# Cross-attention and quantised FFN: FFN bias, residual sum and Wo's low part handed from VectorE to GpSimd

## The reference

```python
x = x + attention(layernorm(x), context) @ Wo + bo
x = x + ffn(layernorm(x))
...
# attention: q = ln(x Wq + bq), k = ln(y Wk + bk), v = y Wv + bv, 16 heads of 32;
# softmax(q k / sqrt(32)) v over 112 keys, plus the same over the 16 dca keys
...
bq = fake_quant(bias, RHS_BITS, -1)
xq = fake_quant(x, LHS_BITS, -1)
kq = fake_quant(kernel, RHS_BITS, 0)
y = jnp.einsum('bsd,df->bsf', xq, kq)
y = y + bq[None, None, :]
y = jax.nn.relu(y)
return fake_quant(y, LHS_BITS, -1)
```

## Time and profile before

| | |
|---|---|
| Time, median of 3 runs | 354.7 us (354.21 to 355.06) |
| Profiled execution | 354.8 us |
| Its span, first to last instruction | 353.0 us |
| Mean granted clock of TensorE | 0.991 |
| PE busy | 321.9 us, 2375 matmuls |
| PEld busy | 254.4 us |
| DVE busy | 315.7 us, 804 instructions |
| ACT busy | 221.9 us, 444 instructions |
| POOL busy | 173.8 us, 261 instructions |

### The profile page before, as it was taken

How to read it: one execution, slowest core, us unless ns; L and a number is a source line. 1 busy time by engine, 2 the same in 40 slices (tenths; PEclk the granted TensorE clock), 3 DMA queues, 4 the chain that set the end, 5 groups by cost and what they waited for, 6 DMA issues and landing times.

```text
span 353.0 us, 7629 instructions
## 1 busy us (share of the span) xinstructions
PE 321.9 (91%) x2375; PEld 254.4 (72%) x2375; DVE 315.7 (89%) x804; ACT 221.9 (63%) x444; POOL 173.8 (49%) x261
## 2 busy tenths in 40 slices
PE   5799989998999999999999999999999999987871
PEld 1355658776788888887878887878787878775630
DVE  3999899998889999999999999999999999986665
ACT  3577886375576767676768585858585856572401
POOL 5211712264373828282828282828383837272720
PEclk9999999999899999999999999999999999999998
DMA  7880345132151514251515151424233313130002
GB/s 268 255 302 3 120 134 185 46 122 78 46 151 46 174 41 153 67 170 49 172 43 178 49 169 58 153 74 147 81 130 97 122 63 121 64 130 22 26 6 89
DMA packets 36451, 38.88 MB, mean 110 GB/s; under 512 B 8760, under 2 KB 27452, under 8 KB 36412
## 3 DMA queue, kind: packets, MB, share of 16 engines
q1 hardware_dynamic: 36044, 38.14, 33.2%
q10 hardware_dynamic: 368, 0.27, 0.3%
HBM read 16.89 MB, written 4.72 MB: 61 GB/s over the span
## 4 chain that ended last, share of the span: by engine, by line
PE 59%; POOL 8%; DVE 7%; issue 5%; ACT 2%; DMA 1%; POOLq 0%; DVEq 0%; ACTq 0%
PE bank L1334 33%; PE bank L1457 9%; POOL finals L536 5%; PE bank L1437 3%; PE bank L1438 3%; PE bank L1629 2%; PE bank L1426 2%; PE bank L1511 2%; PE bank L1516 1%; PE bank L1478 1%; POOL x_small L593 1%; DVE seg_out L1079 1%; PE bank L1619 1%; DVE rden L1073 1%; ACT prob_store L757 1%
## 5 line engine op out<-in xcount | busy, mean ns | idle before, releaser
L517 POOL TENSOR_TENSOR k_lo<-wkv_raw,k_hi 128x448 f16<-128x448 f32 x16 | 16.8, 1049 | 109.4 <-issue 101.5
L1457 PE MATMUL bank<-v_aug,prob_store 128*128 128x66 f32 x512 | 67.1, 274 | 2.1 <-ACT prob_store L757 2.1
L1457 PEld LDWEIGHTS bank<-v_aug,prob_store 128*128 128x128 f32 x512 | 63.1, 191 | 4.5 <-ACT prob_store L757 3.2
L768 ACT ACTIVATE wkv_raw<-bank,affine 128x448 f32<-128x448 f32 (+1 forms) x32 | 22.3, 748 | 40.7 <-PE bank L1511 40.7
L1066 DVE TENSOR_REDUCE neg_max<-bank 128x4 f32<-128x448 f32 (+1 forms) x128 | 44.9, 412 | 0.3 <-PE bank L1426 0.3
L757 ACT ACTIVATE prob_store<-bank,exp_scale 128x512 f32<-128x512 f32 x64 | 41.7, 678 | 4.9 <-PE bank L1438 4.8
L536 POOL TENSOR_TENSOR finals<-seg_out 128x128 f32<-128x128 f32 x64 | 34.5, 548 | 12.6 <-DVE seg_out L1079 12.2
L1437 PE MATMUL bank<-q_stack,k_stack 128*128 128x128 f16 x256 | 33.9, 220 | 0.6 <-ACT maxT L612 0.6
L1438 PE MATMUL bank<-maxT,sel 128*128 128x128 bf16 x256 | 33.7, 219 | 0.0
L1079 DVE TENSOR_TENSOR seg_out<-bank,rden 128x256 f32<-128x256 f32 x64 | 27.2, 425 | 4.0 <-POOL finals L536 1.7
L1437 PEld LDWEIGHTS bank<-q_stack,k_stack 128*128 128x128 f16 x256 | 26.4, 104 | 5.2 <-issue 3.9
(11 more groups left out here) (213 smaller groups left out, 886.2 us busy)
## 6 DMA issues: line engine op xcount, KB each, us to landing
x_in<-in_x SPq DMA_DIRECT2D x16, 256.0 KB, 3.0
q_stack<-q_hi SPq DMA_DIRECT2D x32, 128.0 KB, 2.1
q_stack<-q_lo SPq DMA_DIRECT2D x32, 128.0 KB, 2.1
k_stack<-k_hi SPq DMA_DIRECT2D x32, 128.0 KB, 2.1
k_stack<-k_lo SPq DMA_DIRECT2D x32, 128.0 KB, 2.1
out<-finals SPq DMA_DIRECT2D x16, 256.0 KB, 2.0
y_dcaT<-in_x SPq DMA_DIRECT2D x8, 256.0 KB, 2.8
x_res<-in_x SPq DMA_DIRECT2D x8, 256.0 KB, 2.8
```

The source lines that it names most:

```text
L768: s.activation(n.rearrange("p (c n) -> p c n", n=P)[:, :, 0:keys], src, ACT.Identity, bias=shift, scale=gain).then_inc(n_ready.sem, 1)
L1457: last = mm(bank[6 + gr % 2][:, VW * h:VW * (h + 1)], probs[:, gr % 2, h], v_aug[:, Bt.parity, HG * gr + h], start=True, stop=True)
```

## The change

Three pieces of one-off work go from VectorE to GpSimd or to another place there. `low_output` becomes four subtractions of 128x512 on GpSimd in step 0, behind k's low part of batch 1. Of `setup_ffn_bias`, VectorE keeps the largest magnitude, the scale and its reciprocal and does them in step 1 behind the statistics of the second layer norm instead of ahead of the maxima; GpSimd waits for them (`fbstat_ready`) and does the two 128x512 operations ahead of k's low part of batch 2. The sum of x and the output bias of batch 0 goes from ahead of combine(0) to behind combine(3), on GpSimd as before.

```diff
-        pow2_ready = signal("pow2_ready")
+        pow2_ready, fbstat_ready, fbrnd_ready = signal("pow2_ready"), signal("fbstat_ready"), signal("fbrnd_ready")
...
+            def setup_ffn_bias():
+
+                pool.wait_ge(fbstat_ready.sem, 1)
+                g.tensor_scalar(fb_row[:], fb_row[:], fb_stat[:, 2:3], ROUND, ALU.mult, ALU.add).then_inc(fbrnd_ready.sem, 1)
+                pool.wait_ge(fbrnd_ready.sem, 1)
+                g.tensor_scalar(fb_row[:], fb_row[:], ROUND, fb_stat[:, 1:2], ALU.subtract, ALU.mult
+                                ).then_inc(fbias_ready.sem, 1)
+
+            def low_output():
+                pool.wait_ge(wohi_ready.sem, 1)
+                for c in range(XC):
+                    ins = g.tensor_tensor(wo_lo[:, c], wo_raw[:, c], wo_hi[:, c].bitcast(FP32), ALU.subtract)
+                ins.then_inc(wolo_ready.sem, 1)
...
                         dca_columns(k_hi, kdca_hi)
                         dca_columns(k_lo, kdca_lo)
+                        if C is not None and C.first():
+                            setup_ffn_bias()
                         low(k_lo, k_n, k_hi, kn_ready, khi_ready, kstack_in, klo_ready, MAIN)
+                        if N.second():
+                            low_output()
...
-                if Bt is not None:
+                def residual():
                     if Bt.first():
                         pool.wait_ge(out_bias_ready.sem, 1)
                     pool.wait_ge(*xres_loaded.of(Bt))
                     if Bt.has(1):
                         pool.wait_ge(*x1_ready.of(Bt.back(1)))
                     g.tensor_tensor(x_plus, x_res[Bt.parity], out_bias[:], ALU.add).then_inc(xplus_ready.sem, 1)
+
+                if Bt is not None and not Bt.first():
+                    residual()
...
                     combine(2)
                     combine(3)
+                    if Bt.first():
+                        residual()
...
-            def low_output():
-                dve.wait_ge(wohi_ready.sem, 1)
-                v.tensor_tensor(wo_lo[:], wo_raw[:], wo_hi[:].bitcast(FP32), ALU.subtract).then_inc(wolo_ready.sem, 1)
...
-                link(v.reciprocal(fb_stat[:, 2:3], fb_stat[:, 1:2]))
-                link(v.tensor_scalar(fb_row[:], fb_row[:], fb_stat[:, 2:3], ROUND, ALU.mult, ALU.add))
-                v.tensor_scalar(fb_row[:], fb_row[:], ROUND, fb_stat[:, 1:2], ALU.subtract, ALU.mult
-                                ).then_inc(fbias_ready.sem, 1)
+                v.reciprocal(fb_stat[:, 2:3], fb_stat[:, 1:2]).then_inc(fbstat_ready.sem, 1)
...
                     setup_ffn(0)
                     low_query()
-                    low_output()
...
+                if C is not None and C.first():
+                    setup_ffn_bias()
                 if N is not None and not N.second():
                     low_query()
                 if C is not None and C.first():
...
-                    if C is not None and C.first():
-                        setup_ffn_bias()
                     maxima(0)
                     maxima(1)
```

## The result

The changed kernel takes 360.56 us (median of 4 runs, 359.35 to 361.65), the kernel before 354.88 us (4 runs); the ratio is 1.0162, with a 95% interval of 1.0122 to 1.0202. It is slower, as forecast, but by 5.7 us and not by 1.7, and outside the range. The profiled execution took 359.35 us, the shortest of the four; its span is 357.5 us and its mean granted clock 0.975.

What follows compares the result with a forecast made beforehand. TensorE was taken as busiest, so its waits count. The terms 0 + 0 + 3.7 - 3.56 + 1.5 gave +1.6 to +1.7 on the 354.7 us median: 356.4 us, range 353.2 to 358.2 for 8 in 10.

Steps and rivals of the forecast that it cites:

- step 0: Batch 0 in attention, about 44 to 64 us; Wo's low part moving to GpSimd: 0, bounds -0.8 and +1.5.
- step 1: Pipeline step with batch 1 in attention and batch 0 in the output product, about 64 to 82 us.
- The FFN bias, step 1: GpSimd's wait and wide bias operations ahead of k_lo delay k_raw and TensorE's third weighing: +3.7, bounds +2.1 and +4.2.
- part two 76.65 (+0.56): In step 1, GpSimd's second wide bias operation ends at 76.65, 0.56 us after VectorE's L1030.
- whoever waits comes next: Blocking VectorE and GpSimd instructions in both steps run one after the other, alternating; the waiting engine goes next.
- my race: Step 1's reckoned VectorE and GpSimd alternation: q_lo to 74.45, k_lo to 78.1, L1259 starting at 79.35 instead of 75.63.
- The clock: Behind TensorE's gap of some 4 us in step 1, a new clock fall: +1.5, bounds 0 and +3.
- End of step 1: With no bias for VectorE to make, the ordinary tail runs: -3.56, bounds -3.56 and -2.0.
- rival B: Faster: VectorE and GpSimd don't block each other; 353.2 us, or 352.4 with step 0's 0.8; chance 0.22.
- C: TensorE's gap in step 1 is there but its clock stays at 2.4 GHz: 355.0 us; chance 0.15.
- D: In step 0 GpSimd's four pieces keep VectorE out, k_raw 1.5 late, TensorE waits: 357.9 us; chance 0.11.

Runs made afterwards that it cites:

- add form: The changed kernel, but GpSimd's second bias operation adds -ROUND from a column instead of subtracting the constant; 361.14 us, ratio 1.0148 to the kernel before.
- late wide: The changed kernel, but GpSimd waits for the scale and does both wide bias operations behind combine(3) of step 1; 354.02 us, ratio 0.9925 to the kernel before.
- wait alone: The changed kernel with GpSimd's wait ahead of k_lo kept, but both wide bias operations behind combine(3); 356.86 us, ratio 1.0049 to the kernel before.
- busy gap: The changed kernel plus 20 matmuls of 512 columns into a free bank, ahead of TensorE's third weighing in step 1; 356.91 us, ratio 1.0058 to the kernel before.
- Wo's part alone: The changed kernel with the bias left at VectorE's end of step 1, only Wo's low part and residual sum moved; 354.1 us, ratio 0.9976 to the kernel before.
- early scale: The changed kernel, but VectorE makes the bias scale in step 0 behind q_lo; 352.73 us, ratio 0.9909 to the kernel before; again 353.28 us, 0.9957.
- early scale with Wo undone: The early scale kernel, but Wo's low part and the residual sum as before the change; 356.2 us, ratio 1.0027 to the kernel before.

## Why the prediction was wrong

**What bounds the kernel, and the order of events** held: VectorE idle ahead of its reduction of the centred row, TensorE idle ahead of its third weighing, a fall of the clock, the bias gone from the end of the step. The direction followed. Two terms of the sum were too small. One sign came out by luck: k_raw of step 1 was forecast at 80.4 and stands at 80.33, but the chain ahead of it is 1.3 us longer than forecast and began 1.35 us earlier than before the change (70.25 for 71.60).

**The FFN bias, step 1: +3.7 forecast, +5.03 measured** (chain). The error is one line, "part two 76.65 (+0.56)". I priced both wide operations by L508, and the second, which subtracts a constant and multiplies by a column, is another form: 2.01 us in a place where the first one takes 0.69. With the add form the chain is +3.78, my 3.7. Taken apart by differences between the kernels: the scale ahead of q_lo +0.87 (late wide), GpSimd's wait for it +1.21 (wait alone, 2.08 - 0.87), two wide operations at the ordinary price in front of k_lo +1.70 (add form, 3.78 - 2.08), the slow form +1.25.

The handovers also came in another order than "whoever waits comes next" says. GpSimd's first bias operation waited through q_lo *and* the FFN weights' product (72.49 to 74.63, the product ending at 74.16), which follows q_lo without a break. Between the two, VectorE did not let go. The sum was nearly the same: with the add form k_lo ends 4.48 us behind q_lo's start, and my race has 4.33. GpSimd would have had to wait for the product once in any case.

**The clock: +1.5 forecast, +3.76 measured** (busy gap). I took over the price of the row of before, one stretch of 3.43 us at half clock. But the price is nearly half of the time that TensorE then works at 1.2 GHz, and that was 8.2 us. My upper bound for this term was 3; the six traces with the fall behind this gap give 2.2 to 3.8, so the bound was near, but my own value lies under all of them. Nor does the price follow the gap: 5.47 us cost 3.76, 5.49 us cost 2.22, and 1.36 us cost 3.01.

**End of step 1: -3.56** held. With the clock up, the stretch from the context's transposes to the key transposes is 87.33 to 92.95 in the busy gap, 5.62 us, the ordinary value to the hundredth.

**Step 0: 0 forecast, -0.92 in this trace.** Where the race is lost, my reckoning is right (-0.14 with Wo's part alone, k_raw 0.15 earlier); where it is won, rival B's 0.8 comes, and a little more, though not for B's reason: the engines still block each other (L1047 takes 1.67 us and q_lo 1.79). I had read a race as a rule, from the one time that GpSimd's L583 came first. What I had as hidden stayed hidden: the low queries' transfers, the residual sum and the loads behind it on SyncE.

**The sum.** -0.92 + 5.03 - 3.56 + 3.76 = +4.3, the steps' part of the 4.5 between the profiled spans. The measured +5.7 is between medians: the other three runs are 0.6 to 2.3 us longer than the profiled one, and their excess was not traced, so about 1.2 us of the loss stays open. A second trace of the changed kernel, 2.5 us longer, had its excess outside the two steps. **The rivals.** B is out for step 1, C too (all five traces with a gap over 2 us ahead of the third weighing that was not filled show the fall), D as well. The range was too narrow because each term's bounds came from rows of the same form and the same length as my own value.

The rule of the Trainium skill (SBUF — State Buffer, Who interferes with whom), that the second to issue blocks fully, agrees with L1047's 0.99 and L497's 2.14, which contain the other's rest. It does not foresee that L1046, which started 0.45 us behind L497, got in ahead of it. The Trainium skill's 2.5 cycles per element (GPSIMD Engine Reference, Instruction dispatch) I had misused: the residual sum takes 1.27 to 1.29 us where VectorE does not block it, not the estimated 1.07, but the same addition on 128x128 (combine) takes 0.45, so by estimate 384 elements more cost 0.82 us, 2.6 cycles each at the page's 1.2 GHz. The page's figure agrees, and what I left out is a fixed part of about 0.2 us.

## What to carry to other kernels

Work handed to an idle engine is free only if the engine isn't made to wait for its input ahead of something that others need: move the producer of the input early, or the work late, and look at what is queued behind the wait. Price an operation by a row with the same operators and the same kinds of operands, and if there is none, take a multiple as the upper bound (here the form without a row took three times the one with a row). And a gap in TensorE's work is to be priced with the stretch at half clock that can follow it, for which the whole distance until the clock comes back counts.

## What the runs showed of the hardware

- GpSimd's tensor_scalar on 128x512 float32 depends on its operators and operands: multiply by a column and add a constant 0.69 to 0.70 us; add a column and multiply (the centred row by a constant, the layer norm by a column) 0.68 to 0.77; subtract a constant and multiply by a column 2.01 and 2.04 us. The 2.01 us (late wide) had only PSUM reductions and one small operation of VectorE beside it. During the 2.04 us (early scale, 66.55 to 68.59) a small operation of VectorE (L1061) took 0.57 us instead of 0.19, but the product k_t behind it, two operands in SBUF, began at 67.34 and took 1.08 us, its usual time. So the slow form does not keep VectorE out for its whole length. No trace has a fast form beside the same product.
- Where a GpSimd and a VectorE instruction that block each other start within 0.02 us of each other, either can come first, and the difference on VectorE was 1.1 us (k_raw 5.48 or 6.60 behind L1206).
- TensorE's granted clock fell to half after gaps of 1.23 us (changed kernel, second trace, at 323.50), 1.36 us (late wide), 1.61 us (early scale with Wo undone), 2.57 us (wait alone), 4.29 us (add form) and 5.47 to 5.51 us, but not after 0.80 us (early scale), nor in a gap of 5.7 us of which 20 matmuls filled 4.48, with 1.20 left open. A gap of 1.45 us in step 0 did not bring it down, so the length of the gap alone does not decide.
